# Attention weights of a graph layer held in PSUM in place of SBUF

## What is computed

```python
h = (x @ W).reshape(N, H, C)
a_src = jnp.einsum('nhc,hc->nh', h, att_src)
a_dst = jnp.einsum('nhc,hc->nh', h, att_dst)
e = jax.nn.leaky_relu(a_src[src] + a_dst[dst], NEG_SLOPE)
m = jax.ops.segment_max(e, dst, num_segments=N)
p = jnp.exp(e - m[dst])
denom = jax.ops.segment_sum(p, dst, num_segments=N)
alpha = p / (denom[dst] + 1e-16)
msg = h[src] * alpha[:, :, None]
out = jax.ops.segment_sum(msg, dst, num_segments=N)
```

## Time and profile before

| | |
|---|---|
| median of 3 runs | 4668.64 us (4656.42 to 4673.68) |
| the profiled execution's own time | 4664.53 us |
| its span, first to last instruction | 4662.7 us |
| busy: TensorE, ScalarE, VectorE, GpSimd | 3890.3, 2672.2, 2382.2, 3331.3 us |
| mean granted TensorE clock | 0.798 of 2.4 GHz |

### The profile page before, as it was taken

How to read it: one execution, slowest core, us unless ns; L and a number is a source line. 1 busy time by engine, 2 the same in 40 slices (tenths; PEclk the granted TensorE clock), 3 DMA queues, 4 the chain that set the end, 5 groups by cost and what they waited for, 6 DMA issues and landing times. The chain is left out here.

```text
span 4662.7 us, 130488 instructions
## 1 busy us (share of the span) xinstructions
PE 3890.3 (83%) x40200; PEld 3499.5 (75%) x40201; DVE 2382.2 (51%) x9720; ACT 2672.2 (57%) x4890; POOL 3331.3 (71%) x3234
## 2 busy tenths in 40 slices
PE   3788888888888888887748988999999999899992
PEld 2577777777777777775538888898989888888882
DVE  5522222222222222222757676777777767677767
ACT  3555555555655555563436666666666666666662
POOL 1377777777777777775657777777777777777772
PEclk9799999999899999997867677667776767776766
DMA  3422222222222222222532222222222222222223
GB/s 114 139 54 52 53 54 51 54 52 53 54 51 54 53 52 54 51 53 58 151 99 52 51 51 52 51 53 53 52 53 53 52 51 51 51 52 52 51 51 114
DMA packets 309081, 285.67 MB, mean 61 GB/s; under 512 B 127646, under 2 KB 229812, under 8 KB 309044
## 3 DMA queue, kind: packets, MB, share of 16 engines
q0 software_dynamic: 100352, 160.76, 16.4%
q1 hardware_dynamic: 206786, 121.71, 9.1%
q10 hardware_dynamic: 1906, 2.77, 0.2%
HBM read 249.16 MB, written 35.83 MB: 61 GB/s over the span
## 5 line engine op out<-in xcount | busy, mean ns | idle before, releaser
L655 POOL DMA_INDIRECT a_G<-Htab,a_idx x1568 | 1654.7, 1055 | 494.8 <-issue 477.6
L655 POOL DMA_INDIRECT p_rows<-Btab,p_idx x1568 | 1493.4, 952 | 496.6 <-issue 477.6
L1514 PE MATMUL a_psA<-a_GP,a_S 128*128 128x132 f32 x4704 | 975.9, 389 | 0.7 <-DVE a_GP L1437 0.7
L1514 PEld LDWEIGHTS a_psA<-a_GP,a_S 128*128 128x128 f32 x4704 | 899.4, 290 | 6.5 <-DVE a_GP L1437 0.9
L832 DVE TENSOR_TENSOR p_z<-p_psZ,p_rows 128x512 f32<-128x512 f32 x294 | 198.7, 690 | 1258.6 <-SPq L764 1223.2
L1487 ACT CAST a_S<-a_Sb 128x512 f32<-128x512 bf16 x588 | 633.2, 1130 | 62.2 <-PE a_psA L1514 61.2
L953 PE MATMUL p_psA<-p_msg,p_S 128*128 128x65 f32 x4704 | 599.3, 289 | 21.6 <-ACT p_S L895 21.6
L953 PEld LDWEIGHTS p_psA<-p_msg,p_S 128*128 128x128 f32 x4704 | 581.8, 205 | 25.1 <-issue 25.0
L890 ACT ACTIVATE p_msg<-p_z 128x512 f32<-128x512 f32 x294 | 180.9, 630 | 710.3 <-DVE p_z L832 705.1
L935 PEld LDWEIGHTS p_psZ<-wc,p_s 128*128 128x128 f32 x2352 | 344.2, 213 | 323.2 <-issue 312.9
L895 ACT CAST p_S<-p_Sb 128x1024 f32 (+1 forms) x294 | 550.7, 1972 | 0.0
(11 more groups left out here) (220 smaller groups left out, 5243.1 us busy)
## 6 DMA issues: line engine op xcount, KB each, us to landing
p_ea<-in_ea SPq DMA_DIRECT2D x196, 256.0 KB
p_rows<-Btab,p_idx POOLq DMA_INDIRECT x1568
a_G<-Htab,a_idx POOLq DMA_INDIRECT x1568
Htab<-arena SPq DMA_DIRECT2D x14, 476.0 KB, 3.7
n_x<-in_x SPq DMA_DIRECT2D x14, 448.0 KB, 4.1
hkeep<-n_h SPq DMA_DIRECT2D x14, 448.0 KB, 4.9
hTkeep<-n_hT SPq DMA_DIRECT2D x14, 448.0 KB, 4.1
u_hT<-hTkeep SPq DMA_DIRECT2D x14, 448.0 KB, 4.3
```

The source lines that it names most:

```text
L655: pool.indirect_dma_start(out=rows[:, u * C + c, :], out_offset=None, in_=table, in_offset=bass.IndirectOffsetOnAxis(ap=idx[u][:, c:c + 1] ...
L1514: m = pe.matmul(psA[v][:, 0:HR], S32[v][:, c, :], GP[v][:, c, :], start=c == 0, stop=c == C - 1)
```

## The change

The two SBUF tiles `ep0` and `ep1`, one for even and one for odd steps, are replaced by one PSUM tensor with two halves. The exponential writes to it and the multiplication reads from it. Nothing else differs: no instruction, wait, count or order. The attention pass had seven PSUM banks in use and now has eight.

```diff
-    eq, es, ed, ep = (two(n, [P, C, NH]) for n in ("eq", "es", "ed", "ep"))
+    eq, es, ed = (two(n, [P, C, NH]) for n in ("eq", "es", "ed"))
...
     psN, psE = pst("psN", [P, 512]), pst("psE", [P, 512])
+    ep = pst("ep", [P, 2, C, NH])
...
                         dve.tensor_tensor(GP[u][:, :, :].rearrange("p c (h f) -> p c h f", h=NH),
                                           G[:, slot2, 0:HR].rearrange("p c (h f) -> p c h f", h=NH),
-                                          bc(ep[u][:, :, :], 3, HC + 1), ALU.mult).then_inc(s["GP"], 1)
+                                          bc(ep[:, u, :, :], 3, HC + 1), ALU.mult).then_inc(s["GP"], 1)
...
-                        act.activation(ep[u][:, :, :], ed[u][:, :, :], ACT.Exp).then_inc(s["ep"], 1)
+                        act.activation(ep[:, u, :, :], ed[u][:, :, :], ACT.Exp).then_inc(s["ep"], 1)
```

## The result

The changed kernel takes 4539.88 us (median of 4 runs, 4533.41 to 4541.39) against 4668.33 for the kernel before (4 runs on the same chips): 128 us less, ratio 0.9728 with a 95% interval from 0.9709 to 0.9746. I had predicted 4525. The profiled execution took 4541.14 us with a span of 4539.3.

What follows compares the result with a forecast made beforehand. GpSimd's gathers were taken to bound the attention pass; -148 + 0 + 5 = -143 us takes the profiled execution from 4664.5 to 4521.5, with the runs' median 4.1 us above: 4525 predicted, range 4500 to 4590.

Steps and rivals of the forecast that it cites:

- Part 1: Attention pass's multiplication (L1437): gathers started inside it go from a mean of 1460 to 946 ns, -148 us.
- the margin is used up: Rival: faster gathers uncover slower attention-pass turns; 4% longer gives -129 us, 4540; 6% gives 4578; chance 0.14.
- Part 3: The multiplication's (L1437) own duration stays 1252 ns with weights in PSUM; bounds -10 ns and +1.09 us.
- Part 4: The exponential (L1457), 233 ns, writes to PSUM: from 0.2 us faster to 0.2 slower, both hidden.
- Part 2: One-hot comparison (L1343) still reads two SBUF tiles: its 23 us of holds stay, bounds -13 to +14.
- Part 5: Attention pass's turns, 1926 us against gathers at 1984: margin falls from 206 to 58 us; +5 us for late turns.

## Why the prediction was right, and where its sizes were off

*The bound and the mechanism* were right: the kernel before was bound by gathers, and after the change no gather started in the multiplication is held. Part 1 had -148 us, and 281 gathers at 944 ns say the same. The kernel that writes both places shows that the read makes it. The size was -128 us in place of -143. By its number the rival "the margin is used up" came out (4540) and not the forecast (4525), 15 us apart.

*Part 3* was right: 1250 ns. The Trainium skill ("Perfetto Trace Analysis", section "Optimizing Scalar/DVE Operations") has about 60 ns of overhead for VectorE on SBUF and 125 on PSUM, an estimated 65 ns more; they do not appear in it. *Part 4* was right and hidden.

*Part 2* was mis-sized. I left the comparison's holds at 23 us, in bounds of -13 to +14. They became 240 x (1138 - 944) = 47 us, 24 more. My upper bound took gathers to fall into the comparison by chance (162 of them); they were 240. Gathers and turns are not independent, as the kernels with `iota_nc` in PSUM show. These 24 us alone bring the stream of gathers to where it was measured.

*Part 5* was mis-sized as well. I took the turns' own time as their time less VectorE's waits, 1926 us. With half of the gathers taken away the kernel before (with its masks) needs 6.81 us a turn, 1996 us: 70 more, and more than the 1984 that I had left to the gathers. A wait hides work of others, and subtracting it gives a pace that nobody keeps. The trace of the kernel before bears this out: the 96 turns that follow a wait last 6.31 us without the next wait, the other 196 last 6.72, and in the changed kernel, where almost none follows a wait, they last 6.83. That TensorE and ScalarE catch up while VectorE waits is the likely reason, and was not looked at by itself. My argument against the rival, that a TensorE with less idle time keeps its clock up, found no support: it was busy 97% and not 94% of the 400 us above, at a granted clock of 0.69 in place of 0.70.

The rival "the margin is used up" thus had the turns nearly right: they are 3.6% longer than I had them, and it said -129 for 4%. That -128 came out is partly luck. It knew nothing of the comparison's 24 us, by which the gathers still are no shorter than the turns.

The gathers' stream adds up: it shrank from 2132.3 to 4425.3 + 0.95 - 2421.6 = 2004.7, that is by 127.6. The multiplication gives -148, the comparison +24 and 2 ns less on each of 1568 gathers -3, together -127. The idle time between the gathers did not change, 477.6 and 474.8 + 2.7 us, and the +5 that I took for late turns has no counterpart in the stream.

## What to carry to other kernels

Where GpSimd issues gathers without a pause, look for VectorE instructions that read two SBUF tiles and take more than some 0.13 us: in this kernel each costs a gather that starts in it the time that is left of it, less that 0.13 us. Moving either operand to PSUM frees GpSimd at no price on VectorE, and cutting the instruction in two about halves the loss for 0.07 us more on VectorE. Do not take a loop's own pace as its time less its waits; take the bound away and look. And when a change removes most of a bound, count what the next one gives back.

## What the runs showed of the hardware

- A gather of 128 rows costs GpSimd 0.944 us, and 0.305 us pass before the next, the median in both passes. Started with time t left of a two-SBUF-operand VectorE instruction it takes t + 0.819 us, unless it starts within the first 23 to 44 ns of it, by run, or with less than some 0.13 us left. The Trainium skill ("SBUF — State Buffer", section "A bandwidth-pool intuition that's wrong (but worth ruling out)") says of a DMA beside a VectorE copy that it is "blocked until DVE-end + ~115 ns"; here, beside an operation with two inputs, the block until the end agrees and the figure is another: the gather has 819 of its 944 ns to go when the instruction ends, as if its first 125 ns were not held.
- With either operand in PSUM nothing is held: first operand, fp32, in L832 (68 gathers, 941 to 950 ns); first, bf16, in the comparison (246, 944 ns on average); second, fp32, in the multiplication (281, 944 ns).
- A bf16 comparison of 1024 elements keeps its 691 ns when its first operand is read from PSUM. A 32-element exponential is 25 ns shorter into PSUM (233 to 208); "ScalarE: Activation LUTs" of the Trainium skill ("Step-by-step: what each stage is for") says that ScalarE writes PSUM faster than SBUF, and this row agrees.
